# A first attention body with an order, banks and copies of its own

## The reference

```python
q = x @ Wqa @ Wqb                      # 16 heads, 128 plain + 64 rotary columns
ckv = x @ Wkva                         # compressed (64) and the shared rotary key (64)
kv = compressed @ Wkvb                 # per head: key part (128) and value (128)
q_pe, k_pe = _rope(q_pe), _rope(k_pe)
scores = jnp.einsum('bhnd,bhmd->bhnm', qf, kf) * scale
scores = jnp.where(causal, scores, jnp.finfo(scores.dtype).min)
attn = jax.nn.softmax(scores, axis=-1)
out = jnp.einsum('bhnm,bhmd->bhnd', attn, v)
return out.reshape(b, n, HEADS * VDIM) @ Wout
```

## Time and profile before

| what | value |
|---|---|
| median of three runs | 1778.98 us (1778.82 to 1780.37) |
| profiled execution, its own time | 1779.4 us |
| its span | 1777.6 us |
| TensorE busy | 1698.9 us, 96% of the span |
| VectorE busy | 1241.2 us, 70% |
| ScalarE busy | 985.3 us, 55% |
| GpSimd busy | 561.3 us, 32% |
| mean granted clock of TensorE | 0.988 |

### The profile page before, as it was taken

The page is one execution under the profiler, slowest core; times in us unless marked ns, Lnnn a source line. Parts: engine busy times, 40 slices in busy tenths (PEclk is TensorE's granted clock), DMA queues, the critical chain, the costliest instruction groups (busy, mean ns, idle before and its releaser), DMA issues. The chain is left out here.

```text
span 1777.6 us, 32120 instructions
## 1 busy us (share of the span) xinstructions
PE 1698.9 (96%) x11280; PEld 1389.1 (78%) x11280; DVE 1241.2 (70%) x2864; ACT 985.3 (55%) x2320; POOL 561.3 (32%) x489
## 2 busy tenths in 40 slices
PE   5689999999999999999999999999699999999998
PEld 4567777777777777778777777777489999999998
DVE  6778878887887788878788787876555454554543
ACT  6556666666666666666666666665424333333332
POOL 4444334433344344434443344333201100110100
PEclk9899999999999999999999999999899999999999
DMA  8300000002000002000001100001200000000000
GB/s 279 114 13 7 7 7 13 7 8 95 13 7 7 7 7 102 7 7 7 13 7 59 43 13 7 7 1 37 90 1 25 25 1 24 25 1 25 13 13 13
DMA packets 35805, 51.45 MB, mean 29 GB/s; under 512 B 2305, under 2 KB 26881, under 8 KB 35649
## 3 DMA queue, kind: packets, MB, share of 16 engines
q1 hardware_dynamic: 35648, 49.39, 8.4%
HBM read 35.23 MB, written 14.16 MB: 28 GB/s over the span
## 5 line engine op out<-in xcount | busy, mean ns | idle before, releaser
L1187 ACT ACTIVATE probs<-aps,nmax 128x1024 f32<-128x1024 f32 (+7 forms) x512 | 378.9, 744 | 226.0 <-DVE nmax L1235 220.7
L1235 DVE CUSTOM_DVE_ANT_0 aps<-aps,mask_row 128x1024 f32<-128x1024 f32 (+7 forms) x512 | 388.7, 769 | 143.6 <-PE aps L43 138.2
L1119 PE MATMUL aps<-ident,probs 128*128 128x128 f32 x2304 | 329.5, 273 | 0.6 <-ACT pT L1198 0.6
L43 PE MATMUL aps<-kTh,qh 128*128 128x512 f32 (+3 forms) x768 | 294.3, 383 | 14.1 <-POOL ql L1330 7.7
L1119 PEld LDWEIGHTS aps<-ident,probs 128*128 128x128 f32 x2304 | 272.1, 140 | 22.9 <-issue 1.6
L1198 ACT COPY pT<-aps 128x512 f32<-128x512 f32 (+3 forms) x483 | 233.1, 506 | 90.3 <-PE aps L1119 87.7
L43 PE MATMUL aps<-pT,v 128*64 128x512 f32 (+3 forms) x1536 | 268.9, 492 | 0.8 <-ACT pT L1198 0.8
L43 PE MATMUL aps<-kTl,qh 128*128 128x512 f32 (+3 forms) x768 | 258.3, 344 | 0.0
L43 PE MATMUL aps<-kTh,ql 128*128 128x512 f32 (+3 forms) x768 | 223.9, 346 | 0.0
L1323 POOL TENSOR_TENSOR rot<-rot 64x512 f32<-64x512 f32 x128 | 164.4, 1285 | 186.4 <-DVE rot L1249 186.4
L43 PEld LDWEIGHTS aps<-pT,v 128*64 128x64 f32 x1536 | 101.5, 137 | 152.9 <-issue 142.7
(11 more groups left out here) (177 smaller groups left out, 3043.5 us busy)
## 6 DMA issues: line engine op xcount, KB each, us to landing
wqs<-wq_scratch SPq DMA_DIRECT2D x30, 256.0 KB, 2.7
raw_numbers<-in_x SPq DMA_DIRECT2D x4, 1024.0 KB, 7.2
acc<-in_x SPq DMA_DIRECT2D x8, 512.0 KB, 3.6
x_scratch<-acc SPq DMA_DIRECT2D x8, 512.0 KB, 2.9
x<-x_scratch SPq DMA_DIRECT2D x8, 512.0 KB, 3.9
out<-x SPq DMA_DIRECT2D x7, 512.0 KB, 2.9
heads<-in_heads SPq DMA_DIRECT2D x4, 640.0 KB, 9.8
wout<-in_Wout SPq DMA_DIRECT2D x4, 512.0 KB, 9.7
```

Of the source, the lines that this page charges most:

```text
L43: return nc.tensor.matmul(out, lhsT, rhs, start=start, stop=stop, skip_group_check=True)
L1119: last = nc.tensor.transpose(tps[:, TS.index(x) % 3, j * P:(j + 1) * P], probs[c][:, c * (pair % 2), a, off:off + P], t.ident[:])
L1187: nc.scalar.activation(probs[c][:, c * (r % 2), a, off:off + w], sps[:, at:at + w], ACT.Exp, bias=nmax[:, c, a, j:j + 1], scale=-1.0, accu ...
L1235: nc.vector.tensor_tensor_reduce(out=s, in0=s, in1=mask[:, N - PW[c][j]:N], scale=-1.0, scalar=3.0e38, op0=ALU.add, op1=ALU.min, accum_out ...
```

## The change

Body 0 gets tables of its own: an order for each engine and its own banks. In it Q(1, 1) comes ahead of all scores, the small score tiles (c = 0) come head by head instead of in turns, the large tiles come in another order, PV(0, 0, 4) moves ahead of the last three of them, and every OUT copy is on ScalarE. The other bodies keep theirs. The mask's zeros are now written by GpSimd, and VectorE waits for them and for the DMA ahead of its first MAX instead of its first ROT. The bookkeeping (counts and bank users) follows from the tables of each body.

```diff
+        TENSOR_FIRST = [Q(1, 1), S(0, 1, 0), S(0, 1, 2), S(0, 1, 1), S(0, 1, 3), Q(1, 0), S(0, 0, 0), S(0, 0, 2),
+                        S(0, 0, 1), S(0, 0, 3), S(1, 1, 2), S(1, 1, 0), S(1, 1, 1), T(0, 1, 0), T(0, 0, 1), T(0, 0, 0),
+                        S(1, 1, 3), T(0, 1, 1), T(0, 3, 1), Q(0, 1), L(0), T(0, 2, 0), T(0, 3, 0), T(0, 2, 1),
+                        S(1, 0, 3), Q(0, 0), PV(0, 0, 4), S(1, 0, 0), S(1, 0, 2), S(1, 0, 1)]
...
+        BANK_FIRST = {Q(1, 1): 2, S(0, 1, 0): 1, S(0, 1, 2): 0, S(0, 1, 1): 3, S(0, 1, 3): 1, Q(1, 0): 0,
+                      S(0, 0, 0): 3, S(0, 0, 2): 2, S(0, 0, 1): 1, S(0, 0, 3): 3, S(1, 1, 2): 0, S(1, 1, 0): 2,
+                      S(1, 1, 1): 0, S(1, 1, 3): 2, Q(0, 1): 0, L(0): 1, S(1, 0, 3): 2, Q(0, 0): 0, S(1, 0, 0): 2,
+                      S(1, 0, 2): 0, S(1, 0, 1): 2}
...
-        def body(order, r):
+        def body(order, first, r):
-            return [x for x in order if exists(x, r)]
+            return [x for x in (first if r == 0 else order) if exists(x, r)]
...
         def evac(x, r):
-            return "scalar" if r == LAST else EVAC[x]
+            return "scalar" if r in (0, LAST) else EVAC[x]
...
+        def bank_of(x, r):
+            return (BANK_FIRST if r == 0 else BANK)[x]
...
                 def max_job(x):
                     _, c, a, j = x
-                    at = slot(S(c, a, j)) + place(c, j)
+                    at = slot(S(c, a, j), r) + place(c, j)
+                    if x == VECTOR_FIRST[0] and r == 0:
+                        dve.wait_ge(mask_loaded, 16)
+                        dve.wait_ge(mask_cleared, 1)
...
-                    nc.vector.memset(mask[:, 0:N - P], 0.0)
-                    dve.wait_ge(mask_loaded, 16)
...
+            nc.gpsimd.memset(mask[:, 0:N - P], 0.0).then_inc(mask_cleared, 1)
             nc.gpsimd.memset(ones[:], 1.0)
```

More of the change, by code:

```diff
@@ L937, in attention @@
                 for x in order if x[0] == "out"}
-        LISTS = {"S": SS, "Q": QS, "L": [x for x in TENSOR if x[0] == "l"], "T": TS, "PV": PVS,
-                 "Y": [x for x in TENSOR if x[0] == "y"]}
         KIND = {"s": "S", "q": "Q", "l": "L", "t": "T", "p": "PV", "y": "Y"}
         COUNT = {}
-        for name, xs in LISTS.items():
-            done = [(x, r) for r in BODIES for x in body(xs, r)]
+        for name in KIND.values():
+            done = [(x, r) for r in BODIES for x in tensor_body(r) if KIND[x[0]] == name]
             COUNT.update({(name, x, r): n + 1 for n, (x, r) in enumerate(done)})
         def evac(x, r):
-            return "scalar" if r == LAST else EVAC[x]
+            return "scalar" if r in (0, LAST) else EVAC[x]
         for engine in ("scalar", "vector"):
-            done = [(x, r) for r in BODIES for x in body(TS, r) if evac(x, r) == engine]
+            done = [(x, r) for r in BODIES for x in tensor_body(r) if x[0] == "t" and evac(x, r) == engine]
             COUNT.update({(engine, x, r): n + 1 for n, (x, r) in enumerate(done)})
@@ L960, in out_count, with slot, banks_of @@
             return COUNT[evac(x, r), x, r]
[L962 to L966, removed]
+        def bank_of(x, r):
+            return (BANK_FIRST if r == 0 else BANK)[x]
+        def slot(x, r):
+            return 512 * bank_of(x, r)
+        def banks_of(x, r):
+            return (bank_of(x, r), bank_of(x, r) + 1) if x[0] == "s" and x[1] == 1 else (bank_of(x, r),)
+        USERS = {bank: [(x, r) for r in BODIES for x in tensor_body(r) if x in BANK and bank in banks_of(x, r)]
+                 for bank in range(4)}
         def bank_users(x, r):
             users = set()
[L971 to L979, removed]
+            for bank in banks_of(x, r):
+                n = USERS[bank].index((x, r))
+                users.update(USERS[bank][n - 1:n] if n else [])
             return sorted(users, key=str)
@@ L1079, in q_job @@
                     for wp in range(2):
-                        last = mm(nc, banks[:, BANK[x], :], t.wqs[:, pair % 2, wp, a * P:(a + 1) * P], rhs, wp == 0, wp == 1)
+                        last = mm(nc, banks[:, bank_of(x, r), :], t.wqs[:, pair % 2, wp, a * P:(a + 1) * P], rhs, wp == 0, wp == 1)
                     last.then_inc(q_ps, 1)
@@ L1103, in l_job @@
                     banks_free(x)
-                    at = slot(x)
+                    at = slot(x, r)
                     for j in range(4):
@@ L1163, in run @@
                 job = {"q": q_job, "s": s_job, "l": l_job, "t": t_job, "p": pv_job, "y": y_job, "router": router_job}
-                for x in TENSOR_LAST if r == LAST else body(TENSOR, r):
+                for x in TENSOR_LAST if r == LAST else tensor_body(r):
                     job[x[0]](x)
@@ L1218, in run @@
                 job["router"] = router_job
-                for x in SCALAR_LAST if r == LAST else body(SCALAR, r):
+                for x in SCALAR_LAST if r == LAST else body(SCALAR, SCALAR_FIRST, r):
                     job[x[0]](x)
@@ L1263, in inv_job @@
                     _, c = x
-                    dve.wait_ge(e_done, count([y for y in SS if y[1] == c][-1], r + age(x)))
+                    dve.wait_ge(e_done, max(count(y, r + age(x)) for y in SS if y[1] == c))
                     if exists(L(c), r - 1):
@@ L1305, in run @@
                        "router": router_job}
-                for x in VECTOR_LAST if r == LAST else body(VECTOR, r):
+                for x in VECTOR_LAST if r == LAST else body(VECTOR, VECTOR_FIRST, r):
                     job[x[0]](x)
@@ L1351, in run @@
                 job = {"add": add_job, "low": low_job, "rep": rep_job, "olow": olow_job}
-                for x in body(POOL, r):
+                for x in body(POOL, POOL_FIRST, r):
                     job[x[0]](x)
```

26 lines of the change are left out of this document (20 added, 6 removed).

## The result

The change takes 1784.59 us (median of 11 runs, 1782.5 to 1785.61), the kernel before 1778.95 us (median of 11, 1777.53 to 1780.37): a ratio of 1.0028, 95% interval 1.002 to 1.0036. The difference of the two medians is 5.6 us; the ratios given here, with their intervals, are not quotients of medians, and this one stands for 5.0 us. The change is slower by 0.28%, with an interval that ends at the 0.2% line, and its median is 1.0 us above the top of the predicted range. The profiled execution took 1784.84 us with a span of 1783.0 us, 5.4 us above the span of before.

What follows compares the result with a forecast made beforehand. TensorE bounds attention from the second body on, a four-engine chain the first. Mark 117.45, corrected to 118.0, plus 1.5 for the clock: 119.5, 1.7 us later than before; on median 1778.98 that gives 1780.7 us, range 1778.2 to 1783.6.

Steps and rivals of the forecast that it cites:

- Step 1: Mask's memset and DMA wait leave the first ROT's path: ROT at about 74.15, first scores 79.6 us, 0.9 earlier.
- Step 2: Body 0's small tiles head by head: first large tile S(1,1,2) starts at 90.1 instead of 94.14 us, 4.0 ahead.
- Step 3: Large tiles up to the fifth: waits behind copies and HIGH(0,1) cut the lead to 1.0 us; S(1,0,3) at 105.5 us.
- Step 4: Last three large tiles, then an uncovered wait before body 1's transposes: first score product at 117.45 us, 0.35 ahead.
- the clock term: Half-clock falls at body 0's large tiles: 1.3 us for S(1,0,3) plus 0.2, taken as 1.5; bounds 0 to 6.5.
- general lateness: 0.5 us added to body 1's start, because the same walk over the kernel before gave 117.27 against the trace's 117.81.
- uncorrected walk: Summed chain through body 0 at full clock, without corrections: body 1's first score product at 117.45 against 117.81 us before.
- (a): Rival: slower beyond 0.2%, large tiles at 1.2 GHz cost 1.3 us each; three tiles give 1783.1 us; chance 0.13.
- (b): Rival: faster beyond 0.2%, the 4.0 us lead at S(1,1,2) survives, 1775.0 us; needs both HIGHs 3 us earlier; chance 0.05.
- (d): Rival: the change does what it says but a later body absorbs the shift, 1779.0 us; chance 0.05.
- (c): Rival: no shift, first body bound by the same VectorE and ScalarE work whatever its order, 1779.0 us; chance 0.25.
- my list of what would make the prediction wrong: S(1,0,3) before 103 us, three or more large tiles at 0.50, or bodies from 120 us on taking another time.

## Why the prediction was wrong, step by step

The direction was right, the size was not: +1.7 us forecast, +5.6 measured.

- **Step 1, the mask: right.** First ROT at 74.33 (74.15 predicted), first scores at 79.80 us (79.6). The memset took 0.84 us on GpSimd, inside its bounds, and nothing waited for it.
- **Step 2, the small tiles: right, 0.65 us too early.** 3.4 us of lead where I had 4.0. The kernel with the new start alone keeps 3.7 us of it to the end.
- **Step 3, up to the fifth tile: right in its two waits, wrong in one tile's clock.** The copies ahead of EXP(1, 1, 0), and HIGH(0, 1) ahead of EXP(1, 1, 3), are both there, the latter with a wait of 4.37 us for "some 4". But S(1, 1, 2) ran at 0.52, so S(1, 1, 1) started 5.05 us behind it where I had 3.8. With the waits filled it is 3.94 at the full clock: 1.11 us are the clock.
- **Step 4, the last three: right, with the 2.14 us wait before the transposes.** S(1, 0, 3) ran at 0.51: from its start to S(1, 0, 1)'s it took 9.11 us where I had 7.7. With the waits filled it is 7.85: 1.26 us are the clock.
- **"Two corrections", the clock term: the step that failed.** I took 1.5 us, one fall at a large tile and a little of another. There were three on the chain: 1.11 + 1.26 for the two tiles, and 1.6 behind the mark, which I did not price at all, since I took the bodies from the mark on as unchanged. Together they are 3.97 us. The term's bounds held it (0 to 6.5); I chose the value near the two falls of the trace before, although the stretches of 3.50 and 3.40 us ahead of those two held 1.83 and 1.25 us of work, and the change has one of 4.1 us with nothing in it.
- **"Two corrections", general lateness: too small as well.** I added 0.5 us, from a walk over the kernel before whose working I did not give. What the clock leaves is 1.37 us: 0.65 up to S(1, 1, 2), then 0.04 to 0.20 in each of the five pieces up to the mark. It is a remainder, and no run isolates it.

The whole sum is then -0.36 (the uncorrected walk's 117.45 against 117.81), +1.37, +3.97, which makes the 4.98 us at 158 us.

Of the rivals, (a) named the mechanism and the side, with chance 0.13: three tiles, 1783.1 us. It happened with two tiles and a start of body, so its 1783.1 us is near the 1784.59 partly by luck. Its argument against itself, that work fills 96 to 101 us, did not agree with the forecast's own wait of 96 to 97.8 us. (b)'s 1775.0 us is nearly what the new start gives without the new tail (1775.28), but that is no merit of (b): both HIGHs came later than I had put them, 105.92 us for 103.8 and 115.35 for 111.8. (d) is refuted: later bodies hand the shift on, 4.98 us at 158 us against 5.4 of span. (c) and the forecast itself fall with the clock term. The one thing in my list of what would make the prediction wrong that came true is a body from 120 us on that took another time; only the first did, by 1.6 us. Large tiles at 0.50 were two and a part of a third.

The Trainium skill ("TensorE: Matmul & The Clock Gate", Part 1) says that the same kernel meets the change of clock at other places from run to run. The traces agree as far as they go, with one profile of each kernel: with the mask alone the order of body 0's tiles is that of before, and 87 to 90.5 us has 0.50 for 0.99. The change's own runs spread by 3.1 us and those of before by 2.8 us in the same comparison. So the 1.11, 1.26 and 1.6 us are those of the profiled executions, and others of the same kernel can have other falls.

How sure is the cause? That the tail loses and the start wins is shown by the two halves, which add up to 6.0 of 5.6 us. That the change loses 3.6 us by its slow stretches is shown by filling the waits, and the 1.6 us behind the mark by the two kernels that do without the 2.14 us wait. That the wait for HIGH(0, 1) is a large piece is shown by the swaps, 4.9 us, and in the traces up to the transposes it is the wait itself. These pieces overlap and are not to be added. What stays open is how much of the difference to before is the clock, since the waits of the kernel before were never filled, what makes up the 1.37 us of lateness, and what the order planned for short waits owes to each of its parts.

## What to carry to other kernels

When one engine waits in a chain for others, a wait costs itself and often the slower clock of the work behind it: here 1.1 to 1.6 us for each of the three falls of the change, up to 2.9 us where one lasted longer, and nothing where the chain waited for something else. It can land behind the stretch that was changed, so price the falls on the next body too. In a queue that runs in order, put nothing that waits for a third engine ahead of the instruction that frees TensorE's bank: one such change, a swap on each of two engines, was worth 4.9 us. Before taking over a new order whole, run its halves with the old one: here one half was 3.7 us faster and the other 9.7 us slower.
